# Layer 3's feed-forward: the last two tiles summed by TensorE, and the gate and up loads sent ahead of down's

## Chip, core and metric

The kernel runs on one core of a Trainium2 chip, as one launch. The metric is the device time of one execution in microseconds (us); lower is better.

## What is computed

The reference applies four layers, each with a cross-attention and a feed-forward on the normalised rows, to x of 8 x 100 tokens and 512 features. The change touches the last feed-forward alone. It sends 512 tokens to 4 of 16 experts each (expert numbers and weights are inputs), and adds the experts' weighted outputs to each token:

```python
x = hidden_states.reshape(n_tokens, h)               # 512 tokens, 512 features
flat_expert = topk_idx.reshape(-1)                   # 4 experts of each token
perm = jnp.argsort(flat_expert)
tok = jnp.repeat(jnp.arange(n_tokens), topk)[perm]
xs = x[tok]
gate = ragged_dot(xs, gate_weight^T, group_sizes)    # 16 experts, inner size 352
up = ragged_dot(xs, up_weight^T, group_sizes)
down = ragged_dot(silu(gate) * up, down_weight^T, group_sizes)
out = zeros.at[tok].add(down * w_sorted[:, None])
```

## The kernel before

The program is a chain of eight stages; each engine has one list of instructions, written out in Python, and the engines meet at semaphores. The stage here is class `ChosenFfn`, named `l3f`. Early in the program tables are made that sort the (token, expert) pairs by expert into parts of 64 rows; two parts make a tile of 128 rows, and there are 24 tiles. `rows` holds, for each lane and tile, the token of that lane (or a row beyond the tokens for an empty lane), `rows_f` the same as floats, `slot_weights` the weight.

For tile t:

- POOL gathers the 128 token rows from DRAM (`gather`) into `x_rows`, a ring of 3; TensorE turns them, ScalarE copies them to `x_turned`.
- TensorE makes gate and up for the two halves of 64 lanes, each with its own expert's weights (`pe_gate_up`, L1580), ScalarE the silu, VectorE the product `h`. TensorE turns h (L1597), VectorE copies it, and TensorE makes the down product (`pe_down`, L1607). ScalarE scales it into `y` (L1655), a ring of 2.
- POOL adds the 128 rows of `y` to two arrays in DRAM with indirect DMAs that accumulate (`add_up`, L1541), one for each half of the lanes. An add-up waits until the one before it has landed, since two tiles may add to the same token.

TensorE's list is: gate and up of t, turning of x for t + 1, down of t - 1, turning of h of t.

The weights of the second half's expert are loaded by SP into a ring of 3 (`load_ring`): 1408 KB of gate and up (L1487), 768 KB of down (L1490), from a row that SP reads from a table with `value_load` (L1485). A first half with an expert of its own gets them by POOL's indirect load into one of 2 spare places (`load_spare`, L1497); it is issued for every tile, and rows out of bounds are left out where none is needed. TensorE waits for both before a product.

SP's list in the ring: for each t, fetch the row, wait for gate and up of tile t - 2, load gate and up; wait for down of tile t - 2, load down:

```python
wait(sp, self.s("gate_up_units"), t - self.RING + 2 if t >= self.RING else 0)
sp.dma_start(self.weights[:, q, 0:self.DOWN_AT], ...)
wait(sp, self.s("d_units"), t - self.RING + 2 if t >= self.RING else 0)
sp.dma_start(self.weights[:, q, self.DOWN_AT:self.ROW], ...)
```

POOL's list in the loop: spare gate and up of t + 1, gather of t + 2, add-up of t - 1, spare down of t + 1.

At the end POOL adds up the last tile, SP loads the two arrays of sums (L1526, 1 MB each) into the place of ring 0, TensorE turns them in 32 transposes (L1637), and VectorE adds the eight results to the residual (L1687). SP sends the four pieces out (L4055).

## Time and profile before

| What | Value |
|---|---|
| median of 3 runs | 2156.8 us (2156.68 to 2157.38) |
| the profiled execution, its own time | 2163.69 us |
| its span | 2161.5 us |
| PE busy | 1973.5 us, 91% of the span |
| DVE busy | 1061.3 us, 49% |
| ACT busy | 889.4 us, 41% |
| POOL busy | 567.5 us, 26% |
| chain that ended last | PE 75%, DVE 8%, DMA 7%, ACT 4%, issue 3% |
| of it, loads of l3f gate and up | 4% |
| DMA moved | 189.22 MB, mean 88 GB/s |

The span is the time from the first to the last instruction of the profiled execution. The stage `l3f` is its last part, from some 1880 us on. Busy shares are averages over all eight stages; what limits this stage has to be read from its own windows.

### The profile page before, as it was taken

Reading aid. Unit: us, or ns where it says so; the run is one execution under the profiler, and the core shown is the slowest. Engines: PE = TensorE matmul, PEld = TensorE weight load, DVE = VectorE, ACT = ScalarE, POOL = GpSimd, SP = SyncE. Lnnn points to the kernel's source line nnn. Section 1 sums busy time; section 2 is a strip of 40 time slices with the busy share of each in tenths; the row PEclk is TensorE's granted clock in tenths of the full one; section 3 lists DMA queues with packets and bytes.
Section 4 is the critical chain, followed back from the end, with each engine's and each line's share of the span. In section 5 each row is a group of like instructions: output and inputs, shape, how many; then the busy total and the mean of one; then the engine's idle time right before and its main releaser. Section 6 shows DMA issues by size and latency. Waiting matters only on the chain.

```text
span 2161.5 us, 38438 instructions
## 1 busy us (share of the span) xinstructions
PE 1973.5 (91%) x14580; PEld 1560.8 (72%) x14580; DVE 1061.3 (49%) x2477; ACT 889.4 (41%) x1819; POOL 567.5 (26%) x416
## 2 busy tenths in 40 slices
PE   6989999996997999986899999999999999798886
PEld 6977777885446878774587777999989999633333
DVE  5546666764114366688747777333234555410111
ACT  4346666532223455566655544422253232211110
POOL 3333332322342211000031110333241110145553
PEclk9999999998998999997999999999999999899998
DMA  3200010238355221141020000222220000468895
GB/s 125 77 25 29 14 42 5 70 126 310 71 88 126 76 83 55 66 157 44 5 72 34 29 15 3 89 62 58 68 77 24 29 28 2 169 193 258 264 279 154
DMA packets 67918, 189.22 MB, mean 88 GB/s; under 512 B 15114, under 2 KB 16366, under 8 KB 62510
## 3 DMA queue, kind: packets, MB, share of 16 engines
q1 hardware_dynamic: 50606, 163.90, 22.5%
q0 software_dynamic: 17152, 23.10, 5.6%
q8 instruction: 110, 1.80, 0.3%
q14 instruction: 50, 0.41, 0.1%
HBM read 224.56 MB, written 20.91 MB: 114 GB/s over the span
## 4 chain that ended last, share of the span: by engine, by line
PE 75%; DVE 8%; DMA 7%; ACT 4%; issue 3%; SPq 1%; POOL 1%; ACTq 0%; DVEq 0%; POOLq 0%
PE psum L106 16%; PE psum L109 15%; PE psum L107 15%; DMA l3f_weights<-in_l3f_gate_up_dram 4%; PE psum L1580 4%; PE psum L900 3%; PE psum L3610 3%; PE psum L3578 2%; PE psum L2801 2%; PE psum L3596 2%; PE psum L1607 2%; PE psum L926 2%; PE psum L2447 1%; PE psum L3032 1%; PE psum L139 1%
## 5 line engine op out<-in xcount | busy, mean ns | idle before, releaser
L1580 PE MATMUL psum<-l3f_weights,l3f_x_turned 128*64 (+1 forms) x768 | 131.0, 498 | 30.6 <-issue 16.6
L1580 PEld LDWEIGHTS psum<-l3f_weights,l3f_x_turned 128*64 128x64 f32 x768 | 58.1, 148 | 94.2 <-issue 72.3
L2238 ACT ACTIVATE l2x_probs<-psum,l2x_shift 100x361 f32<-100x361 f32 x128 | 70.2, 562 | 97.3 <-DVE l2x_shift L2293 97.3
L1875 POOL TENSOR_TENSOR l2x_ctx_lo<-l2x_ctx_raw,l2x_ctx_hi 128x1448 fp32r<-128x1448 f32 x8 | 26.4, 3297 | 314.9 <-ACT l2x_ctx_hi L1883 314.9
L1676 DVE TENSOR_TENSOR l3f_h<-l3f_silu,psum 128x352 f32<-128x352 f32 x24 | 12.5, 522 | 164.4 <-ACT l3f_silu L1662 156.0
L3749 ACT ACTIVATE l0x_probs<-l0x_probs,l0x_lowest 100x361 f32<-100x361 f32 x128 | 75.2, 588 | 42.1 <-DVE l0x_lowest L3918 42.1
L106 PE MATMUL psum<-xn_hi,l2f_w_gu_hi 128*128 128x400 f32 x256 | 88.6, 346 | 1.6 <-DVE xn_lo L192 1.3
L448 POOL TENSOR_TENSOR l2f_w_gu_lo<-l2f_raw_gu,l2f_w_gu_hi 128x512 fp32r<-128x512 f32 x32 | 43.0, 1357 | 174.2 <-ACT l2f_w_gu_hi L463 174.2
L107 PE MATMUL psum<-xn_lo,l2f_w_gu_hi 128*128 128x400 f32 x256 | 87.8, 343 | 0.0
L2476 ACT ACTIVATE ln_squares<-l1x_clipped,l1x_key_shift,l1x_key_scale 128x400 f32<-128x400 f32 (+1 forms) x96 | 62.3, 712 | 51.4 <-DVE l1x_clipped L2515 51.4
L3918 DVE CUSTOM_DVE_ANT_0 l0x_probs<-psum,l0x_outside 100x361 f32<-100x361 f32 x128 | 62.9, 531 | 32.1 <-PE psum L3578 29.6
L900 PE MATMUL psum<-l0f_weights,l0f_x_turned 128*128 x160 | 74.3, 608 | 1.2 <-ACT l0f_x_turned L1042 0.8
L1662 ACT ACTIVATE l3f_silu<-psum 128x352 f32<-128x352 f32 x24 | 11.1, 464 | 154.8 <-PE psum L1580 145.3
L647 DVE TENSOR_TENSOR l2f_h<-l2f_silu,psum 128x800 f32<-128x800 f32 x16 | 15.8, 988 | 119.1 <-PE psum L109 119.1
L3610 PE MATMUL psum<-ln_squares,l0x_l_turned 128*128 128x400 f32 (+1 forms) x192 | 73.0, 516 | 0.0
L2838 ACT ACTIVATE ln_squares<-psum 64x64 f32<-64x64 f32 x128 | 28.0, 219 | 106.5 <-PE psum L2801 104.2
L109 PE MATMUL psum<-xn_hi,l2f_w_gu_lo 128*128 128x400 f32 x256 | 68.5, 344 | 0.0
L1607 PE MATMUL psum<-l3f_weights,l3f_h_turned 128*64 (+1 forms) x288 | 67.0, 600 | 0.9 <-DVE l3f_h_turned L1682 0.9
L1875 POOL TENSOR_TENSOR l1x_ctx_lo<-l1x_ctx_raw,l1x_ctx_hi 128x1448 fp32r<-128x1448 f32 x8 | 26.5, 3310 | 134.7 <-ACT l1x_ctx_hi L1883 134.7
L1875 POOL TENSOR_TENSOR l3x_ctx_lo<-l3x_ctx_raw,l3x_ctx_hi 128x1448 fp32r<-128x1448 f32 x8 | 26.4, 3295 | 126.3 <-ACT l3x_ctx_hi L1883 126.3
L2289 DVE TENSOR_REDUCE l2x_highest<-psum 100x2 f32<-100x722 f32 x64 | 57.9, 904 | 0.1
L1541 POOL DMA_INDIRECT l3f_sum_dram<-l3f_y,l3f_rows x24 | 35.0, 1460 | 86.3 <-ACT l3f_y L1655 65.7
(553 smaller groups left out, 6120.9 us busy)
## 6 DMA issues: line engine op xcount, KB each, us to landing
l3f_weights<-in_l3f_gate_up_dram SPq DMA_DIRECT2D x24, 1408.0 KB
l3f_weights<-in_l3f_down_dram SPq DMA_DIRECT2D x24, 768.0 KB
l0x_w_raw<-in_slabs_dram SPq DMA_DIRECT2D x52, 256.0 KB, 2.6
l0f_weights<-in_slabs_dram SPq DMA_DIRECT2D x8, 1536.0 KB
l1x_piece<-in_bit_w_dram SPq DMA_DIRECT2D x8, 1024.0 KB, 6.4
l1f_raw<-in_bit_w_dram SPq DMA_DIRECT2D x8, 1024.0 KB, 8.3
l2f_raw_gu<-in_slabs_dram SPq DMA_DIRECT2D x32, 256.0 KB, 2.6
l0x_ctx_raw<-in_ctx_dram SPq DMA_DIRECT2D x8, 724.0 KB, 4.2
```

The source lines that it names most:

```text
L106: pe.matmul(outs[i], weight_hi, moving[i][0], start=first, stop=False)
L107: pe.matmul(outs[i], weight_hi, moving[i][1], start=False, stop=False)
L109: mm = pe.matmul(outs[i], weight_lo, moving[i][0], start=False, stop=last)
L900: mm = pe.matmul(c.psum[:, t % 2, :], self.x_turned[:, t % 2, k, :], self.weights[:, bass.DynSlice(expert, 1), k * 512:(k + 1) * 512].rear ...
L1580: mm = pe.matmul(c.psum[lanes, bank + x, 0:self.INNER], self.x_turned[:, t % 2, k, lanes], weights, start=k == 0, stop=k == KD - 1)
L1607: mm = pe.matmul(c.psum[lanes, 6 + t % 2, :], self.h_turned[:, t % 2, k, lanes], weights, start=k == 0, stop=k == 2)
L1875: pool.tensor_tensor(self.ctx_lo[:, q, :, :], self.ctx_raw[:, :, :], self.ctx_hi[:, q, :, :], ALU.subtract).then_inc(self.s("ctx_split"), 1)
L2238: act.activation(self.probs[:, m % 2, g, :], c.psum[0:S, g, 0:C], ACT.Exp, bias=self.shift[:, g:g + 1], scale=self.SCALE, accum_out=self.t ...
L2476: act.activation(self.exps(c, m)[0:z - a, t, :], self.clipped[0:z - a, t, :], ACT.Exp, bias=shift, scale=scale).then_inc(self.s("exps"), 1)
L3610: mm = pe.matmul(c.psum[:, 6, 0:4 * S], self.l_turned[0:z - a, q, t, :], turned[0:z - a, t, :], start=t == 0, stop=t == 2)
L3749: act.activation(self.probs[:, g, :], self.probs[:, g, :], ACT.Exp, bias=self.lowest[:, g:g + 1], scale=-1.0, accum_out=self.total[:, g:g ...
L3918: dve.tensor_tensor_reduce(self.probs[:, g, :], c.psum[0:S, g, 0:C], self.outside[:, q, :], -self.SCALE, 3.0e38, ALU.add, ALU.min, self.lo ...
```

## The change

- `load_ring` is split. The gate and up load of tile t + 1 is now sent before the down load of tile t, and so is the fetch of its row number. The first three tiles, loaded ahead, keep their order.
- `ADDED` = 22: POOL adds up tiles 0 to 21 only. The last two tiles' `y` stay in SBUF. For each of them VectorE makes a table of zeros and ones (`places_of_row`): lane by token, one where the lane holds that token. TensorE multiplies `y` by it, which sums the lanes of a token and turns the result at once, into the four PSUM banks of the output.
- The arrays of sums are loaded once the add-ups of 22 tiles have landed, into a buffer of their own (`sums`), not into ring 0; the wait for the last down product is gone. VectorE joins the two arrays (4 adds of 128 x 512), TensorE multiplies the joined sums by the identity (16 matmuls) and accumulates them in the same banks. VectorE then has four adds to the residual in place of eight.

```diff
--- before.py
+++ after.py
@@ -1222,6 +1222,7 @@
     WIDE = 2 * INNER
     DOWN_AT, ROW = KD * WIDE, KD * WIDE + 3 * D
     RING, SPARE, ROWS = 3, 2, 3
+    ADDED = TILES - 2
     INNER_TILES = [(0, P), (P, 2 * P), (2 * P, INNER)]
     ROUND = 1.5 * 2.0 ** 23
 
@@ -1240,9 +1241,9 @@
         self.silu, self.h = (c.sb(own, n + x, [P, 2, self.INNER]) for x in ("_silu", "_h"))
         self.h_turned = c.sb(own, n + "_h_turned", [P, 2, 3, P])
         self.y = c.sb(own, n + "_y", [P, 2, D])
-        c.sb(own, n + "_behind_the_output_weights", [P, 5504])
+        sums = c.sb(own, n + "_sums", [P, 5504])
         self.weights = c.sb(own, n + "_weights", [P, self.RING + self.SPARE, self.ROW])
-        self.sums = self.weights[:, 0, 0:2 * self.groups * D].rearrange("p (x g d) -> p x g d", x=2, g=self.groups)
+        self.sums = sums[:, 0:2 * self.groups * D].rearrange("p (x g d) -> p x g d", x=2, g=self.groups)
 
     def early_buffers(self, c, ctx):
 
@@ -1479,13 +1480,19 @@
                            self.tile_values[:, x, :, :].rearrange("p x t -> p (x t)"), start=x == 0, stop=x == n - 1)
         mm.then_inc(c.sem("table_units"), 1)
 
-    def load_ring(self, c, sp, t):
+    def ring_row(self, sp, t):
+        return sp.value_load(self.ring_rows[0:1, t:t + 1], min_val=0, max_val=P * (self.experts - 1))
+
+    def load_gate_up(self, c, sp, t, at):
 
         q = t % self.RING
-        at = sp.value_load(self.ring_rows[0:1, t:t + 1], min_val=0, max_val=P * (self.experts - 1))
         wait(sp, self.s("gate_up_units"), t - self.RING + 2 if t >= self.RING else 0)
         sp.dma_start(self.weights[:, q, 0:self.DOWN_AT],
                      c.a["l3f_gate_up"][bass.DynSlice(at, P), :]).then_inc(self.s(f"gate_up_landed{q}"), 16)
+
+    def load_down(self, c, sp, t, at):
+
+        q = t % self.RING
         wait(sp, self.s("d_units"), t - self.RING + 2 if t >= self.RING else 0)
         sp.dma_start(self.weights[:, q, self.DOWN_AT:self.ROW],
                      c.a["l3f_down"][bass.DynSlice(at, P), :]).then_inc(self.s(f"down_landed{q}"), 16)
@@ -1508,7 +1515,9 @@
         sp.wait_ge(c.sem("tables"), 4)
         sp.dma_start(self.second_rows[:, :], self.rows[self.PART:P, :]).then_inc(self.s("second_rows"), 16)
         for t in range(self.RING):
-            self.load_ring(c, sp, t)
+            at = self.ring_row(sp, t)
+            self.load_gate_up(c, sp, t, at)
+            self.load_down(c, sp, t, at)
         for b in range(4):
             self.write_rows(c, sp, b)
 
@@ -1518,11 +1527,16 @@
             self.write_rows(c, sp, b)
         sp.dma_start(c.out[:, :, self.tokens:T], c.residual[:, :, self.tokens:T]).then_inc(c.sem("out_written"), 16)
         sp.wait_ge(self.s("x_landed0"), 16)
+        at = self.ring_row(sp, self.RING)
+        self.load_gate_up(c, sp, self.RING, at)
         for t in range(self.RING, self.TILES):
-            self.load_ring(c, sp, t)
-        sp.wait_ge(self.s("d_units"), self.TILES)
+            this, at = at, None
+            if t + 1 < self.TILES:
+                at = self.ring_row(sp, t + 1)
+                self.load_gate_up(c, sp, t + 1, at)
+            self.load_down(c, sp, t, this)
         for x in range(2):
-            sp.wait_ge(self.s(f"added_up{x}"), 16 * self.TILES)
+            sp.wait_ge(self.s(f"added_up{x}"), 16 * self.ADDED)
             sp.dma_start(self.sums[:, x, :, :], self.sum_drams[x][0:self.tokens, :].rearrange(
                 "(g p) d -> p g d", g=self.groups)).then_inc(self.s(f"sum_landed{x}"), 16)
 
@@ -1556,11 +1570,10 @@
                 self.load_spare(c, pool, t + 1, 0)
             if t + 2 < self.TILES:
                 self.gather(c, pool, t + 2)
-            if t:
+            if 0 < t <= self.ADDED:
                 self.add_up(c, pool, t - 1)
             if t + 1 < self.TILES:
                 self.load_spare(c, pool, t + 1, 1)
-        self.add_up(c, pool, self.TILES - 1)
 
     def halves(self, t, place, at, n):
 
@@ -1629,14 +1642,21 @@
             before = place
         self.pe_down(c, pe, self.TILES - 1, before)
         pe.wait_ge(self.s("h"), self.TILES)
+        pe.wait_ge(self.s("y"), self.ADDED + 1)
+        pe.wait_ge(self.s("places_of_row"), 1)
+        for m in range(KD):
+            pe.matmul(c.psum[:, m, :], self.y[:, self.ADDED % 2, m * P:(m + 1) * P], self.x_rows[:, 0, :], start=True,
+                      stop=False)
+        for g in range(self.groups):
+            pe.wait_ge(self.s("sums_joined"), g + 1)
+            for m in range(KD):
+                pe.matmul(c.psum[:, m, g * P:(g + 1) * P], self.sums[:, 0, g, m * P:(m + 1) * P], c.identity[:, :],
+                          start=False, stop=False)
         pe.wait_ge(self.s("y"), self.TILES)
-        for x in range(2):
-            pe.wait_ge(self.s(f"sum_landed{x}"), 16)
-            for m in range(KD):
-                for g in range(self.groups):
-                    mm = pe.transpose(c.psum[:, 4 * x + m, g * P:(g + 1) * P], self.sums[:, x, g, m * P:(m + 1) * P],
-                                      c.identity[:, :])
-                mm.then_inc(self.s("sum_units"), 1)
+        pe.wait_ge(self.s("places_of_row"), 2)
+        for m in range(KD):
+            pe.matmul(c.psum[:, m, :], self.y[:, (self.ADDED + 1) % 2, m * P:(m + 1) * P], self.x_rows[:, 1, :],
+                      start=False, stop=True).then_inc(self.s("sum_units"), 1)
 
     def act(self, c, act):
         act.wait_ge(c.sem("residual_ready"), self.index + 1)
@@ -1666,6 +1686,15 @@
                 out(t - 1)
         out(self.TILES - 1)
 
+    def places_of_row(self, dve, t):
+
+        into = self.x_rows[:, t - self.ADDED, :]
+        dve.wait_ge(self.s("x_units"), t)
+        for g in range(self.groups):
+            op = dve.tensor_scalar(into[:, g * P:(g + 1) * P], self.lane_ids, self.rows_f[:, t:t + 1], -float(g * P),
+                                   ALU.subtract, ALU.is_equal)
+        op.then_inc(self.s("places_of_row"), 1)
+
     def dve(self, c, dve):
         half_dve(self.norm, dve, 1)
         n = self.INNER_TILES[2][1] - self.INNER_TILES[2][0]
@@ -1680,12 +1709,17 @@
             c.apart(dve)
             dve.tensor_copy(self.h_turned[:, t % 2, 0:2, :].rearrange("p k l -> p (k l)"), c.psum[:, 5, 0:2 * P])
             dve.tensor_copy(self.h_turned[0:n, t % 2, 2, :], c.psum[0:n, 5, 2 * P:3 * P]).then_inc(self.s("h_turned"), 1)
-        for u in range(2 * KD):
-            dve.wait_ge(self.s("sum_units"), u + 1)
-            wait(dve, self.s("first_added"), u - KD + 1)
-            into = c.residual[:, u % KD, 0:self.tokens]
-            dve.tensor_tensor(into, into, c.psum[:, u, 0:self.tokens], ALU.add).then_inc(
-                self.s("first_added" if u < KD else "added"), 1)
+            if t + 1 >= self.ADDED and t + 1 < self.TILES:
+                self.places_of_row(dve, t + 1)
+        for x in range(2):
+            dve.wait_ge(self.s(f"sum_landed{x}"), 16)
+        for g in range(self.groups):
+            dve.tensor_tensor(self.sums[:, 0, g, :], self.sums[:, 0, g, :], self.sums[:, 1, g, :], ALU.add).then_inc(
+                self.s("sums_joined"), 1)
+        for m in range(KD):
+            dve.wait_ge(self.s("sum_units"), m + 1)
+            into = c.residual[:, m, 0:self.tokens]
+            dve.tensor_tensor(into, into, c.psum[:, m, 0:self.tokens], ALU.add).then_inc(self.s("added"), 1)
         dve.wait_ge(self.s("added"), KD)
         dve.nop().then_inc(c.sem("residual_ready"), 1)
```

SP, the end of the ring and the loads of the sums, before (`in_l3f_gate_up_dram` and `in_l3f_down_dram` are the weights). The `ISA` rows hold the waits; `TENSOR_LOAD` is the fetch of the row number.

```order
L1487 ISA
L1487 DMA l3f_weights<-in_l3f_gate_up_dram 128x2816
L1490 ISA
L1490 DMA l3f_weights<-in_l3f_down_dram 128x1536
L1485 TENSOR_LOAD l3f_ring_rows
L1485 ISA x2
L1487 ISA
L1487 DMA l3f_weights<-in_l3f_gate_up_dram 128x2816
L1490 ISA
L1490 DMA l3f_weights<-in_l3f_down_dram 128x1536
L1526 DMA l3f_weights<-l3f_sum_dram 128x4x512 x2
```

The same place now:

```order
L1497 ISA
L1497 DMA l3f_weights<-in_l3f_down_dram 128x1536
L1484 TENSOR_LOAD l3f_ring_rows
L1484 ISA x2
L1490 ISA
L1490 DMA l3f_weights<-in_l3f_gate_up_dram 128x2816
L1497 ISA
L1497 DMA l3f_weights<-in_l3f_down_dram 128x1536
L1497 ISA
L1497 DMA l3f_weights<-in_l3f_down_dram 128x1536
L1540 DMA l3f_sums<-l3f_sum_dram 128x4x512 x2
```

Each gate and up load, with its fetch, now stands ahead of the down load of the tile before it, and two down loads stand at the end.

TensorE, from the last down product (L1607) to the end, before:

```order
L1607 ISA
L1607 MATMUL psum<-l3f_weights,l3f_h_turned 64x512 x2
L1607 ISA
L1607 MATMUL psum<-l3f_weights,l3f_h_turned 64x512 x2
L1607 ISA
L1607 MATMUL psum<-l3f_weights,l3f_h_turned 64x512 x2
L1637 MATMUL psum<-identity,l3f_weights 128x128 x32
```

The same place now (down product L1620):

```order
L1620 ISA
L1620 MATMUL psum<-l3f_weights,l3f_h_turned 64x512 x2
L1620 ISA
L1620 MATMUL psum<-l3f_weights,l3f_h_turned 64x512 x2
L1620 ISA
L1620 MATMUL psum<-l3f_weights,l3f_h_turned 64x512 x2
L1648 MATMUL psum<-l3f_x_rows,l3f_y 128x512 x4
L1653 MATMUL psum<-identity,l3f_sums 128x128 x16
L1658 MATMUL psum<-l3f_x_rows,l3f_y 128x512 x4
```

The 32 transposes have become 4 matmuls on 512 columns, 16 on 128 and 4 on 512.

VectorE, the last two tiles and the adds, before:

```order
L1681 COPY l3f_h_turned<-psum 128x256
L1682 COPY l3f_h_turned<-psum 96x128
L1676 TENSOR_TENSOR l3f_h<-l3f_silu,psum 128x352
L1681 COPY l3f_h_turned<-psum 128x256
L1682 COPY l3f_h_turned<-psum 96x128
L1687 TENSOR_TENSOR residual<-residual,psum 128x512 x8
```

The same place now, from the table for tile 22 on:

```order
L1694 TENSOR_SCALAR l3f_x_rows<-l3f_constants,l3f_rows_f 128x128 x4
L1705 TENSOR_TENSOR l3f_h<-l3f_silu,psum 128x352
L1710 COPY l3f_h_turned<-psum 128x256
L1711 COPY l3f_h_turned<-psum 96x128
L1694 TENSOR_SCALAR l3f_x_rows<-l3f_constants,l3f_rows_f 128x128 x4
L1705 TENSOR_TENSOR l3f_h<-l3f_silu,psum 128x352
L1710 COPY l3f_h_turned<-psum 128x256
L1711 COPY l3f_h_turned<-psum 96x128
L1717 TENSOR_TENSOR l3f_sums<-l3f_sums 128x512 x4
L1722 TENSOR_TENSOR residual<-residual,psum 128x512 x4
```

The tables stand behind the copies of h of tiles 21 and 22, the joins behind the last copies, and four adds follow in place of eight.

## Rows read from the trace of the kernel before

**Rows 1.** Chain of waits, in order of time: start us, us, what.

```profile
2102.91 0.87 issue
2103.79 4.95 PE psum L1580 x32
...
2109.32 2.75 PE psum L1607 x12
...
2113.32 11.21 DMA l3f_weights<-in_l3f_gate_up_dram
2124.53 0.82 issue
2125.35 7.33 PE psum L1580 x32
```

**Rows 2.** TensorE timeline, gate and up: start us, us, operation, idle before.

```profile
1904.96 4.95 PE L1580 MATMUL psum<-l3f_weights,l3f_x_turned 128*64 x32
1913.63 4.95 PE L1580 MATMUL psum<-l3f_weights,l3f_x_turned 128*64 x32
1925.41 6.61 PE L1580 MATMUL psum<-l3f_weights,l3f_x_turned 128*64 x32 [3.04 <-issue]
...
2092.41 4.95 PE L1580 MATMUL psum<-l3f_weights,l3f_x_turned 128*64 x32
...
2112.49 4.96 PE L1580 MATMUL psum<-l3f_weights,l3f_x_turned 128*64 x32
```

**Rows 3.** Windows: us; busy PE, PEld, DVE, ACT, POOL; clock; DMA share; GB/s.

```profile
1913.80:2125.30 211.50, 182.15 (x1020) 77.28 (x1018) 23.41 (x62) 35.18 (x61) 119.38 (x101) 0.96 0.86 265
2110.50:2113.00 2.50, 2.50 (x15) 0.94 (x13) 0.29 (x1) 0.69 (x1) 0.00 (x0) 1.00 0.46 118
1914.00:1925.40 11.40, 8.38 (x51) 3.47 (x47) 1.64 (x5) 1.75 (x3) 6.59 (x6) 1.00 0.97 300
```

**Rows 4.** Waits from 1900 to 2130 us: total us, times, longest us.

```profile
PE psum L1580 <- issue: 16.3, 8, 3.0
...
PE psum L1580 <- DMA l3f_weights<-in_l3f_gate_up_dram: 13.1, 5, 4.1
```

**Rows 5.** Timeline of POOL: add-ups (L1541) and spare loads (L1497).

```profile
1905.57 1.46 POOL L1541 DMA_INDIRECT l3f_sum_dram<-l3f_y,l3f_rows  x1 [8.18 <-ACT l3f_y L1655]
...
1910.42 1.03 POOL L1497 DMA_INDIRECT l3f_weights<-in_l3f_gate_up_dram,l3f_spare_rows  x1 [0.30 <-issue]
...
2102.75 1.46 POOL L1541 DMA_INDIRECT l3f_sum_dram<-l3f_y,l3f_rows  x1 [2.57 <-DMA l3f_sum_dram<-l3f_y,l3f_rows]
...
2113.06 1.46 POOL L1541 DMA_INDIRECT l3f_sum_dram<-l3f_y,l3f_rows  x1 [3.15 <-ACT l3f_y L1655]
...
2117.91 1.03 POOL L1497 DMA_INDIRECT l3f_weights<-in_l3f_gate_up_dram,l3f_spare_rows  x1 [0.30 <-issue]
```

**Rows 6.** Chain of waits, the end of the program.

```profile
2140.52 3.67 DMA l3f_sum_dram<-l3f_y,l3f_rows
...
2144.26 7.07 DMA l3f_weights<-l3f_sum_dram
...
2158.28 0.68 DVE residual L1687
```

**Rows 7.** Timeline of the end: last down product.

```profile
2136.67 2.79 PE L1607 MATMUL psum<-l3f_weights,l3f_h_turned 128*64 x12 [0.94 <-DVE l3f_h_turned L1682]
```

**Rows 8.** Tile l3f_weights: landing of the two loads of sums.

```profile
DMA to landing us min/median/max: 7.1/7.5/7.9
```

**Rows 9.** Costliest groups of the page: xcount, busy us, mean ns, idle.

```profile
L900 PE MATMUL psum<-l0f_weights,l0f_x_turned 128*128 x160 | 74.3, 608 | 1.2 <-ACT l0f_x_turned L1042 0.8
```

**Rows 10.** Source line 1478: ns min, median, max; first and last start us.

```profile
L1478 PE MATMUL psum<-l0x_q_latent x32: 203/275/275, 63.8 to 67.2; 128*128 128x48 f32 x32
```

**Rows 11.** Groups by form on VectorE: xcount, busy us, mean ns, idle us.

```profile
L1687 DVE TENSOR_TENSOR residual<-residual,psum 128x512 f32<-128x512 f32 x8 | 5.4, 686 | 17.0 <-PE psum L1637 16.9
...
L1421 DVE TENSOR_SCALAR l0x_q_latent<-l0x_q_latent,l3f_constants 128x96 f32<-128x96 f32 x4 | 0.8, 266 | 0.0
```

## The prediction

> **What bounds the kernel now.** I read the chain of waits first. In layer 3's feed-forward the chain runs gate and up product, down product, gate and up load, next product; after the last tile it runs add-ups in DRAM, load of the sums, turning, adds [rows 1, 6]. The reader should see two separate places: a loop of tiles, and a tail.
>
> The loop. The product of tile 3 starts at 1913.63 and that of tile 23 at 2125.35 [rows 1, 2]: 211.7 us for 20 tiles, 10.59 each. A tile that waits for nothing takes 8.67 (1904.96 to 1913.63 [rows 2]). Of the 1.92 lost per tile, TensorE's idle time before the products is 16.3 + 13.1 = 29.4 us in all [rows 4]; most of the rest is products that took 6.6 to 7.3 us in place of 4.95 after an idle time [rows 1, 2]. The windows give a mean granted clock of 0.96 and a DMA share of 0.86 over these 211.5 us [rows 3]. So the DMA engines have 0.86 x 211.5 = 182 us of work, 9.1 per tile, and are idle 1.5 per tile. Neither engine nor DMA is full; the loop is made of latencies.
>
> Two chains could close it. (a) SP: the product of tile 21 ends at 2108.74 (2103.79 + 4.95), but the gate and up load of tile 23, which waits for no more than that, goes out at 2113.32, because SP first stands at the wait of down's load of tile 22 for the down product of tile 20, and then fetches an address: 4.6 us late. It lands at 2124.53 and the product starts at 2125.35 [rows 1]. Meanwhile the DMA share is 0.46 from 2110.5 to 2113 [rows 3]: 1.35 us idle. (b) POOL: tile 20's add-up goes out at 2113.06, 9.27 after the start of tile 21's product; behind it in POOL's queue is the spare gate and up load of tile 23, at 2117.91, for which TensorE waits too [rows 5]. The view names the SP load, but leaves 0.8 us of "issue" behind its landing [rows 1], so POOL's own landing may well be the last. From the add-up to the product, X, it takes 2125.35 - 2113.06 = 12.3 us. For the pair before, the add-up at 2102.75 and the product at 2112.49 [rows 2, 5], X = 9.7. With little on the DMA queues (add-up of tile 0 at 1905.57, product of tile 3 at 1913.63 without a wait [rows 2, 5]) X is at most 8.1. Over the loop two tiles take 21.2 = 9.27 + 11.9, so X is 11.9 on average, waits for earlier add-ups included.
>
> **The change, part by part.**
>
> Gate and up ahead of down, 20 tiles. No instruction is added; the load goes out up to 4.6 us earlier, the address fetch falls behind down's load, where SP has time. Down's load goes out when it did, and may land later by what is left of the gate load in front of it; it is not needed until a whole further product has run, over 8 us. (a) is gone. (b) remains, and is late next: POOL's order, its waits and its transfers are unchanged; only what they meet changes. Bounds: nothing gained if X stays 11.9 (10.59 per tile); at the other end TensorE's 8.67, or 38.3 us over 20 tiles; DMA work of 9.1 per tile stops it at 211.7 - 182 = 29.7 us. I take X = 9.7, since in that pair the gate load was already on its way when the add-up went out, as it always will be: (9.27 + 9.7) / 2 = 9.5 per tile, 190 us. **Gain 21.7 us.** The products at a low clock are in that, since the gaps before them shrink.
>
> Here a rule speaks against the change. In the trace X grows from at most 8.1 to 12.3 between few and many SP transfers. The Trainium skill, DMA: Bandwidth & Descriptors, section "Queues, rings and completion order", says that each DMA engine takes turns between rings only after a whole packet of one ring. By that rule an SP ring that is never empty makes POOL's add-ups wait for a packet at each turn; that is the second rival below.
>
> The tail. I call T the start of tile 23's product. Now the span ends 2161.5 - 2125.35 = 36.15 after T. Removed: two tiles' add-ups (four indirect DMAs), the wait for them, half of the turning (32 transposes), four of eight adds. Added: 8 table instructions on VectorE, at 266 ns for 96 columns [rows 11] some 1.1 us per tile; VectorE idles there until the next tile's silu, so they cost nothing; without that cover they would delay a tile by 1.1. On the path after it:
> - The product, down of tile 22, and down of tile 23 end at 2139.46 [rows 7] = T + 14.1, of which 2.4 is the low clock of 7.33 against 4.95 [rows 1]: T + 11.7.
> - Tile 22's rows enter by 4 matmuls of 128x128 on 512 columns. Nearest row: 160 records, 74.3 us, 20 tiles of 4 such matmuls [rows 9]: 3.7 us. T + 15.4.
> - The sums must be there. Tile 21's add-up goes out at T - 9.5 + 9.27 = T - 0.2, its second half 1.7 later, lands 3.67 after issue [rows 6] plus some 1.2 for down's load beside it: T + 6.4. The loads take 7.1 to 7.9 [rows 8]: T + 14.3. Four joins on VectorE at the adds' 0.69 [rows 11]: T + 15.0 to T + 17.1, beside TensorE's work.
> - 16 matmuls of 128 columns: 32 records in 3.6 us for 48 columns [rows 10], so 0.23 or a little more each, 3.8: T + 19.2.
> - 4 more matmuls on 512 columns for tile 23: 3.7, T + 22.9. One add behind, 0.8: T + 23.7. From the last add's end (2158.96 [rows 6]) to the end of the span 2.5: T + 26.2.
>
> **Gain 36.15 - 26.2 = 9.9 us**, 7.5 where the last product stays at the low clock. Bounds: 6, if the sums land 3 to 4 us later; 12, if the 128-column matmuls run as fast as weight loads allow.
>
> **Sum.** 21.7 + 9.9 = 31.6. The profiled execution took 2163.7 (span 2161.5); it becomes 2132.1. The median of the runs, 2156.8, is 6.9 lower: **2125 us.**
>
> **The rivals.**
> 1. Order pays in full: the DMA engines never idle, 9.1 per tile. For it: they carry 0.97 where both loads are queued, at 300 GB/s [rows 3]. Against: POOL's X would have to fall to 8.9. 29.7 + 9.9: 2117 us; with TensorE as the bound 2109.
> 2. Order pays nothing: X stays 11.9, since POOL's add-ups and the spare load behind them end the loop, not SP's load. For it: the 0.8 us behind the landing [rows 1], and POOL's own wait for an add-up of 2.57 us [rows 5]. The tail alone gives 7.5: 2149 us. This is what the rule above would make of it.
> 3. Slower: the gate load of the next tile now gets ahead of POOL's transfers once more per turn, and X grows by it. Price: 1408 KB at 300 GB/s [rows 3] is 4.8 us, for each of 10 pairs of tiles 48, less the tail's 7.5: 2197 us. It decides from 0.75 us per pair. Against: the bytes per tile are the same, and the DMA engines have 1.5 us per tile free.
>
> **How the numbers follow.** A measurement of this kernel can tell 0.2%, 4.3 us. My forecast 0.57, rival 1 0.18, rival 2 0.2, rival 3 0.05. The range reaches from between the two values of rival 1, 2111, to rival 2 with its tail, 2149. Faster by over 0.2% are all but rival 3 and its mild forms: 0.93; within 0.2% 0.03; slower 0.04.
>
> **What would show it.** SP's gate load goes out within 0.5 us after a product's end; starts of products 9.5 apart; DMA share over the loop about 0.95 and no window like 2110.5 to 2113; low-clock products rare. If the starts stay 10.4 or more apart with POOL's add-ups 12 us ahead of the product, rival 2 holds. In the tail: the loads of the sums issued before TensorE ends tile 23, the first join near T + 15, the end near T + 26. It is wrong if a down product waits for its load, or if the joins start after T + 19.

## The result, and the profile after

The changed kernel takes 2174.8 us (median of 6 runs, 2164.8 to 2178.9), the kernel before on the same chip 2156.7 (6 runs, 2155.5 to 2157.4): 1.0063 times as long, with a 95% interval of 1.0037 to 1.0088. (The ratios here and below are estimated over all runs; that of the two medians is 1.0084.) I had forecast 2125, faster. The profiled execution took 2176.7 us, its span is 2174.9, 13.4 longer than before.

The window over the loop, from the start of tile 3's product to that of tile 23, answers to [rows 3]; the second window runs from POOL's last load for tile 21 to the start of its product, the third covers that product, the fourth the 3.2 us ahead of tile 23's. Columns: us; busy PE, PEld, DVE, ACT, POOL; clock; DMA share; GB/s.

```profile
1918.85:2147.10 228.25, 190.30 (x1020) 79.93 (x1020) 23.02 (x62) 34.63 (x60) 115.49 (x98) 0.90 0.74 234
2119.70:2127.40 7.70, 3.32 (x18) 1.10 (x17) 1.14 (x3) 1.30 (x3) 5.26 (x5) 0.88 0.87 298
2127.40:2134.80 7.40, 7.40 (x33) 3.19 (x34) 0.00 (x0) 0.00 (x1) 2.66 (x3) 0.67 0.43 101
2143.90:2147.10 3.20, 3.20 (x17) 1.07 (x15) 0.52 (x1) 0.95 (x3) 1.01 (x1) 1.00 0.09 9
```

The 20 tiles take 228.3 us, 11.4 each, against 211.7 before and 190 forecast. The DMA share fell from 0.86 to 0.74, and the clock from 0.96 to 0.90. The DMA engines do not stand still while TensorE waits (0.87 in the second window); their idle time comes in the product behind the wait (0.43), since SP's next gate and up load has to wait for the end of that late product. TensorE's wait and POOL's, from 1915 to 2150 us (total us, times, longest), answer to [rows 4]:

```profile
POOL l3f_sum_dram L1555 <- ACT l3f_y L1675: 91.3, 21, 10.2
...
PE psum L1593 <- issue: 41.0, 10, 6.4
```

The waits that carried the name of SP's gate and up load are gone. What is left carries no DMA's name, and is longer than the two kinds of before together: without tile 3's own 3.0 it is 38.0 us in 9 waits, against 29.4 in 13. Of these nine the chain of waits shows two (start us, us, what):

```profile
2099.10 3.71 issue
2102.81 7.71 PE psum L1593 x32
...
2122.99 4.38 issue
2127.37 7.38 PE psum L1593 x32
```

Every second tile waits, and most products after a wait run part of the time at the lower clock, 1.2 GHz (mean granted clock 0.67 from 2127.40 to 2134.80): seven of them take 6.3 to 7.7 us in place of 4.95. These seven cost 16.3 us; the four of before cost 7.9. So the difference of the spans closes: loop 16.6 (8.6 more waiting and 8.4 more of low clock, less 0.4 that these rows leave open), tile 3 later by 5.2 (3.0 is a wait that it did not have, 2.1 came in ahead of the stage), tail shorter by 8.4. 16.6 + 5.2 - 8.4 = 13.4.

What TensorE waits for is seen by setting three engines side by side. SP, then POOL, then TensorE, timelines of the last waiting pair:

```profile
2110.71 0.33 SPq L1490 DMA_DIRECT2D l3f_weights<-in_l3f_gate_up_dram  x1
2114.02 0.33 SPq L1497 DMA_DIRECT2D l3f_weights<-in_l3f_down_dram  x1
2119.38 0.33 SPq L1490 DMA_DIRECT2D l3f_weights<-in_l3f_gate_up_dram  x1
2122.69 0.33 SPq L1497 DMA_DIRECT2D l3f_weights<-in_l3f_down_dram  x1
2134.93 0.33 SPq L1490 DMA_DIRECT2D l3f_weights<-in_l3f_gate_up_dram  x1
```

```profile
2114.85 1.47 POOL L1555 DMA_INDIRECT l3f_sum_dram<-l3f_y,l3f_rows  x1 [8.06 <-ACT l3f_y L1675]
2116.62 1.43 POOL L1555 DMA_INDIRECT l3f_sum_dram<-l3f_y,l3f_second_rows  x1 [0.31 <-issue]
2118.36 1.04 POOL L1504 DMA_INDIRECT l3f_weights<-in_l3f_down_dram,l3f_spare_rows  x1 [0.30 <-issue]
2119.71 1.01 POOL L1504 DMA_INDIRECT l3f_weights<-in_l3f_gate_up_dram,l3f_spare_rows  x1 [0.31 <-issue]
...
2128.38 1.01 POOL L1504 DMA_INDIRECT l3f_weights<-in_l3f_gate_up_dram,l3f_spare_rows  x1 [0.30 <-issue]
...
2143.93 1.01 POOL L1504 DMA_INDIRECT l3f_weights<-in_l3f_gate_up_dram,l3f_spare_rows  x1 [0.30 <-DMA l3f_sum_dram<-l3f_y,l3f_rows]
```

```profile
2114.24 4.95 PE L1593 MATMUL psum<-l3f_weights,l3f_x_turned 128*64 x32
...
2127.37 7.38 PE L1593 MATMUL psum<-l3f_weights,l3f_x_turned 128*64 x32 [4.38 <-issue]
...
2147.14 4.95 PE L1593 MATMUL psum<-l3f_weights,l3f_x_turned 128*64 x32
```

The product that waits is tile 21's (2127.37; tiles 22 and 23 start at 2138.47 and 2147.14). Its gate and up load by SP went out at 2110.71, 16.7 us earlier. What is young is POOL's spare gate and up load for tile 21, at 2119.71, 7.7 us ahead. And 0.33 us ahead of it stands SP's load of 1408 KB for tile 22, whose product starts only at 2138.47. This 0.33 is no accident: SP's load waits for the end of tile 20's product (2114.24 + 4.95), POOL's comes 4.86 after an add-up, and that add-up follows the down product just ahead of tile 20's product. So the two meet in the same way ahead of eight of the nine waits, 0.31 to 0.33 us apart (2048.91 and 2049.24, 2069.45 and 2069.78). Ahead of the ninth, tile 11's and the longest (6.4 us), SP's load goes out at 2003.76, within the 1.01 us of POOL's instruction from 2003.73. Before, SP's last gate load stood 4.6 us ahead of POOL's spare load (2113.32 and 2117.91 [rows 1, 5]).

The same rows say why only every second tile waits. POOL's spare load for tile 22 needs nothing of the late product and goes out at 2128.38; SP's load for tile 23 has to wait for the end of the late product and follows 6.6 us later, at 2134.93. In the ten tiles between the waits it follows 2.6 to 8.4 us later, and no product waits. Tile 23 is the test of this: there is no tile 24, so no gate and up load meets its spare load at 2143.93, the DMA share is 0.09, and the product starts on time at 2147.14. The spare load had landed after 3.2 us at most; in the nine waits it was 6.2 to 9.7 us old when the product began.

The tail, timeline of TensorE and of the joins (T is 2147.14):

```profile
2157.20 2.80 PE L1620 MATMUL psum<-l3f_weights,l3f_h_turned 128*64 x12 [2.05 <-DMA l3f_weights<-in_l3f_down_dram,l3f_spare_rows]
2159.93 3.70 PE L1648 MATMUL psum<-l3f_x_rows,l3f_y 128*128 128x512 f32 x8
2163.47 3.73 PE L1653 MATMUL psum<-identity,l3f_sums 128*128 128x128 f32 x32
2167.04 3.60 PE L1658 MATMUL psum<-l3f_x_rows,l3f_y 128*128 128x512 f32 x8
```

```profile
2160.82 2.50 DVE L1717 TENSOR_TENSOR l3f_sums<-l3f_sums 128x512 f32<-128x512 f32 x4 [4.88 <-DMA l3f_sums<-l3f_sum_dram]
...
2170.67 0.69 DVE L1722 TENSOR_TENSOR residual<-residual,psum 128x512 f32<-128x512 f32 x1 [0.17 <-PE psum L1658]
```

The span ends at T + 27.8 (36.15 before, 26.2 forecast). The tables of ones took 0.93 and 1.04 us for four and lay beside other work.

### The profile page after: what moved, and what is told of

It is laid out like the page before. It is cut to its first block, busy times and chain, and to the rows that moved or that the text cites. A ratio compares the mean times of both kernels' runs of the same rounds, so it can differ in the third digit from the quotient of the medians.

```text
span 2174.9 us, 38469 instructions
## 1 busy us (share of the span) xinstructions
PE 1984.8 (91%) x14596; PEld 1562.7 (72%) x14596; DVE 1063.5 (49%) x2485; ACT 889.3 (41%) x1819; POOL 562.5 (26%) x412
## 4 chain that ended last, share of the span: by engine, by line
PE 79%; DVE 8%; ACT 4%; issue 4%; DMA 3%; SPq 1%; POOL 1%; POOLq 0%; ACTq 0%; DVEq 0%
PE psum L106 16%; PE psum L109 14%; PE psum L107 14%; PE psum L1593 6%; PE psum L900 3%; PE psum L3644 3%; PE psum L1620 3%; PE psum L3612 2%; PE psum L2835 2%; PE psum L3630 2%; PE psum L926 2%; PE psum L3066 1%; PE psum L2481 1%; DMA l0f_weights<-in_slabs_dram 1%; PE psum L139 1%
## 5 line engine op out<-in xcount | busy, mean ns | idle before, releaser
L1593 PE MATMUL psum<-l3f_weights,l3f_x_turned 128*64 (+1 forms) x768 | 137.0, 516 | 42.2 <-issue 41.3
L1705 DVE TENSOR_TENSOR l3f_h<-l3f_silu,psum 128x352 f32<-128x352 f32 x24 | 12.5, 521 | 180.1 <-ACT l3f_silu L1682 180.1
L1620 PE MATMUL psum<-l3f_weights,l3f_h_turned 128*64 (+1 forms) x288 | 67.0, 600 | 2.0 <-DMA l3f_weights<-in_l3f_down_dram,l3f_spare_rows 2.0
## 6 DMA issues: line engine op xcount, KB each, us to landing
l0f_weights<-in_slabs_dram SPq DMA_DIRECT2D x8, 1536.0 KB, 17.5
```

The lines of the kernel that those rows point to most:

```text
L1593: mm = pe.matmul(c.psum[lanes, bank + x, 0:self.INNER], self.x_turned[:, t % 2, k, lanes], weights, start=k == 0, stop=k == KD - 1)
L1620: mm = pe.matmul(c.psum[lanes, 6 + t % 2, :], self.h_turned[:, t % 2, k, lanes], weights, start=k == 0, stop=k == 2)
```

## The experiments

Two theories stood after the result. **A**: POOL's spare gate and up load, behind the add-ups in POOL's list, is what TensorE waits for; the new SP order puts another tile's load in front of it. **The rival**: the loop is slower for another reason that came with the change (the tail's part of it, SP's own transfers, or TensorE's clock). Other letters in the expectations stand for forms of this rival. All runs are compared with the kernel before on their own chip, whose medians were 2157.7, 2158.3 and 2160.5 us. Brackets behind a ratio hold its 95% interval.

### The two halves of the change apart

SP's new order alone, on the kernel before with its old tail (the loop; `load_ring` is split as in the change):

```diff
-        for t in range(self.RING, self.TILES):
-            self.load_ring(c, sp, t)
+        at = self.ring_row(sp, self.RING)
+        self.load_gate_up(c, sp, self.RING, at)
+        for t in range(self.RING, self.TILES):
+            this, at = at, None
+            if t + 1 < self.TILES:
+                at = self.ring_row(sp, t + 1)
+                self.load_gate_up(c, sp, t + 1, at)
+            self.load_down(c, sp, t, this)
```

> The changed order of SP's loads alone, with the old tail. Theory A (the gate load of tile t + 1 goes out just ahead of POOL's spare gate load for tile t, which carries no weights in nearly every tile but whose landing TensorE waits for, and which now lands only with that gate load): the loop is as slow as in the changed kernel, product of tile 23 some 228 us after that of tile 3 (211.7 before), low-clock products 7 or so; total 2174.8 + 8.4 = about 2183 us. Theory B (the loss comes from the new buffer, tables or tail, not the order): about 2157 us. Theory C (rival 2 of the prediction, the order neither helps nor hurts): 2157 us as well.

Measured: 2185.4 us (4 runs, 2182.1 to 2193.0), ratio 1.0129 [1.0099, 1.0159]. The loop, 1918.00 to 2147.66, takes 229.7 us:

```profile
1918.00:2147.60 229.60, 188.67 (x1020) 79.49 (x1020) 22.17 (x58) 34.57 (x60) 115.63 (x98) 0.90 0.74 233
```

```profile
PE psum L1594 <- issue: 43.9, 10, 6.4
```

Clock, DMA share and waits are those of the changed kernel (43.9 us with tile 3's own 3.0 us, as 41.0 there). The whole loss is the order's: 27.8 us of the medians on one chip.

The new tail alone, with SP's old order:

```diff
-        at = self.ring_row(sp, self.RING)
-        self.load_gate_up(c, sp, self.RING, at)
         for t in range(self.RING, self.TILES):
-            this, at = at, None
-            if t + 1 < self.TILES:
-                at = self.ring_row(sp, t + 1)
-                self.load_gate_up(c, sp, t + 1, at)
-            self.load_down(c, sp, t, this)
+            at = self.ring_row(sp, t)
+            self.load_gate_up(c, sp, t, at)
+            self.load_down(c, sp, t, at)
```

> The changed tail alone: the last two tiles summed by TensorE, loads of gate and up and down in the old order. Theory A: loop as before (211 to 213 us from the product of tile 3 to that of tile 23), the tail 7.5 to 9.9 us shorter, total 2147 to 2149 us. Theory B: the loop is slow here too, product of tile 23 over 220 us after that of tile 3, total about 2175 us.

Measured: 2154.7 us (10 runs, 2146.3 to 2161.9), ratio 0.9992 [0.9977, 1.0008]: less than expected. The profiled execution was the shortest one, 2146.3, with a loop of 204.4 us (1913.00 to 2117.35, before 211.7) and a tail of T + 27.15. So the tail is as short as in the changed kernel in this trace, but the ten times lie up to 15.6 us apart, which buries a gain of 8 us. That it is the loop which differs from run to run is not shown: one execution has a trace. The tail's worth can't be read from this pair.

### POOL's spare load moved, under both SP orders

The spare gate and up load and the gather go out one tile earlier, ahead of the add-up. The spare load for tile t + 2 takes the place of tile t's, so it waits there for tile t's product:

```diff
+        self.load_spare(c, pool, 1, 0)
+        self.gather(c, pool, 2)
         for t in range(self.TILES):
-            if t + 1 < self.TILES:
-                self.load_spare(c, pool, t + 1, 0)
             if t + 2 < self.TILES:
-                self.gather(c, pool, t + 2)
+                self.load_spare(c, pool, t + 2, 0)
+            if t + 3 < self.TILES:
+                self.gather(c, pool, t + 3)
             if 0 < t <= self.ADDED:
                 self.add_up(c, pool, t - 1)
```

> The changed kernel, with POOL's spare gate load and gather one step earlier in its list: the spare gate load of tile t + 2 and the gather of tile t + 3 stand ahead of the add-up of tile t - 1 (each still waits for the product or turning that frees its place). Theory A: the spare gate load no longer stands behind the add-ups and behind the gate load of the next tile; it lands beside its own tile's gate load, 5 us or more before it is needed. The loop falls to 8.9 to 9.5 us per tile, product of tile 23 178 to 190 us after tile 3; total 2125 to 2137 us. If instead the DMA engines' work or the add-ups' chain bounds the loop (rival D), it stays above 10 us per tile and the total above 2147 us.

Measured: 2119.3 us (4 runs, 2117.5 to 2122.0), ratio 0.9819 [0.9799, 0.9839]. Better than expected: the products of tiles 3 to 23 start 8.67 us apart without a wait.

```profile
1913.60:2087.20 173.60, 173.58 (x1023) 73.92 (x1022) 23.65 (x64) 35.02 (x61) 116.03 (x97) 1.00 0.99 313
```

```profile
2079.11 1.47 POOL L1555 DMA_INDIRECT l3f_sum_dram<-l3f_y,l3f_rows  x1 [2.12 <-ACT l3f_y L1677]
...
2088.40 1.45 POOL L1555 DMA_INDIRECT l3f_sum_dram<-l3f_y,l3f_rows  x1 [4.74 <-ACT l3f_y L1677]
2090.15 1.42 POOL L1555 DMA_INDIRECT l3f_sum_dram<-l3f_y,l3f_second_rows  x1 [0.30 <-issue]
2091.88 1.05 POOL L1504 DMA_INDIRECT l3f_weights<-in_l3f_down_dram,l3f_spare_rows  x1 [0.30 <-issue]
```

The first fence is the window over the loop: TensorE is busy throughout at a clock of 1.00. The second is the end of POOL's timeline; the down product of tile 23 waits 2.9 us for the last spare load in it, 2091.88, behind an add-up again.

The two loads still meet. In this trace SP's gate and up load goes out 0.3 to 1.0 us ahead of POOL's spare load in each tile from tile 5 on (2066.30 and 2066.97, for one), as in the changed kernel. But that spare load belongs to the tile after next: its product starts 11.5 us later, where TensorE came to the nine waits of the changed kernel 3.3 us after the spare load went out. What pays is the lead, not that the meeting is avoided.

The same POOL list with SP's old order:

> The changed tail, SP's loads in the old order, and POOL's spare gate load and gather one step earlier. Theory A: what is left is SP's own late gate load (4.6 us behind the product), which lands 9 to 11 us after its issue; the loop gains little over the old one, 9.9 to 10.4 us per tile, total 2133 to 2146 us, slower than the same list of POOL with the new order of SP. Rival D (DMA work or the add-ups bound the loop): the same time as the changed tail alone, 2148 us.

Measured: 2137.1 us (4 runs, 2134.5 to 2140.2), ratio 0.9902 [0.9879, 0.9925], 9.48 us per tile (189.6 from 1914.01 to 2103.58), less than the 9.9 expected at least.

```profile
1914.00:2103.60 189.60, 174.72 (x1023) 75.16 (x1022) 25.02 (x70) 35.29 (x61) 115.88 (x97) 1.00 0.95 291
```

```profile
PE psum L1591 <- issue: 14.6, 14, 1.8
```

Here the waits that I had called chain (a), SP's late gate load, are what is left: 14 of at most 1.8 us. The view gives them no name; ahead of the last, at 2103.58, SP's load went out 9.7 us before and POOL's spare load 13.5. With the new tail throughout, the four kernels are:

| | SP old order | SP new order |
|---|---|---|
| POOL's spare load behind the add-up | 2154.7 | 2174.8 |
| POOL's spare load ahead of it | 2137.1 | 2119.3 |

The same edit of SP's list costs 20 us in one row and gains 18 in the other (three of the four were measured on one chip, 2174.8 on that of the result; with the old tail the loss is 27.8 us on one chip). The spare load's place decides its sign.

### Nothing moved, but SP's load held back

If it is the meeting of two loads 0.33 us apart that costs, holding SP's back a little must help. In the changed kernel the gate and up load of tile t got one wait more, on the copy of the turned x:

```diff
+        wait(sp, self.s("x_turned"), t if t > self.RING else 0)
```

> The changed kernel, but SP's gate load of tile t also waits for ScalarE's copy of the turned x of tile t - 1, which ends some 1.3 us after the product it waited for. Everything else, the place ahead of down's load too, is as in the changed kernel. Theory A (what costs is that the gate load is issued 0.3 us ahead of POOL's empty spare load and is served first, 2119.38 against 2119.71 us in the changed kernel's trace): now the spare load is issued about 1 us ahead of it; part or all of the delay goes, the loop falls from 11.4 to between 9 and 10.6 us per tile, total 2120 to 2158 us. Rival E (an earlier gate load slows POOL's transfers by sharing the DMA engines with them, whichever comes first): 1 us later changes little, 11.0 us per tile or more, total 2166 us or more.

Measured: 2143.6 us (10 runs, 2132.0 to 2158.3), ratio 0.9925 [0.9894, 0.9957]. In the trace, of the slowest of these runs, POOL's load now goes out first, at 2100.93, and SP's 1.3 us behind it. The third row is the product for which that spare load is:

```profile
2100.93 1.01 POOL L1505 DMA_INDIRECT l3f_weights<-in_l3f_gate_up_dram,l3f_spare_rows  x1 [0.30 <-issue]
```

```profile
2102.20 0.01 SPq L1491 DMA_DIRECT2D l3f_weights<-in_l3f_gate_up_dram  x1
```

```profile
2108.43 7.17 PE L1594 MATMUL psum<-l3f_weights,l3f_x_turned 128*64 x32 [4.22 <-issue]
```

So going out first by 1.3 us is not enough by itself: the product still waits 4.2 us, and its spare load is 7.5 us old. In this trace ten spare loads have SP's load 0.9 to 1.3 us behind them. Four had landed after 4.0 us or less; six were 5.3 to 8.8 us old when their product ended its wait. That chance may be why the ten times lie 26 us apart, which one trace cannot show.

And held back until the down product, which is 3.5 us after the product's end in the trace (4.6 in the kernel before, 0.2 in the changed one):

```diff
+        wait(sp, self.s("d_units"), t - self.RING + 1 if t > self.RING else 0)
```

> The changed kernel, but SP's gate load of tile t also waits for the down product of tile t - 3, the wait that down's load of tile t - 1 has; gate load first, down's load right behind. The gate load goes out 3.3 us after the product, against 4.6 before the change and 0.2 in the changed kernel. Theory A: the spare load is ahead of the gate load in most pairs of tiles; loop 9.3 to 10.4 us per tile, total 2126 to 2153 us. Rival E: between before and the changed kernel, about 11 us per tile, total near 2165 us.

Measured: 2146.7 us (10 runs, 2144.1 to 2153.7), ratio 0.9946 [0.9929, 0.9963]. SP's load goes out 3.0 us or more behind POOL's, and the 14 waits, of at most 2.6 us, end on spare loads 4.4 to 6.3 us old. Issuing a load later made the kernel 31 and 28 us faster by the medians (on two chips whose kernels before differ by 1.6 us), which no theory gives in which SP's own loads were what TensorE waited for.

### The spare loads left out

For tiles 1 to 23 the spare loads and TensorE's waits for them are gone, and with them the weights of a first half that has an expert of its own:

> The changed kernel without POOL's spare loads (gate and up, and down) for tiles 1 to 23 and TensorE's waits for them; those of tile 0 stay. It leaves out the weights of a first half with an expert of its own, where a tile has one. Theory A: the loop is free of the only late landing, 8.7 to 9.2 us per tile; total 2112 to 2128 us. Rival E or the add-ups' chain as the bound: the add-ups, the gather and both loads of SP are unchanged, so the loop stays above 10 us per tile, total above 2145 us.

Measured: 2118.5 us (4 runs, 2116.0 to 2120.7), ratio 0.9814 [0.9774, 0.9854]. SP's order, the add-ups and the gathers are those of the changed kernel, though on POOL the gathers no longer have spare loads ahead of them:

```profile
1913.90:2087.30 173.40, 173.40 (x1021) 73.83 (x1020) 23.61 (x64) 34.87 (x61) 76.06 (x59) 1.00 0.97 314
```

How much those loads carry is in the page's part on DMA queues (packets, MB, share), first of the kernel with POOL's list moved, which still has them all, then of this one:

```profile
q0 software_dynamic: 16832, 22.58, 5.5%
```

```profile
q0 software_dynamic: 10208, 22.55, 5.5%
```

46 loads less take away 6624 packets, 144 each, and 0.03 MB. With these inputs the spare loads carry next to nothing. What was expensive was waiting for their completion, not sending them: the version with POOL's list moved sends all of them and is as fast.

### What the tail is worth on a loop without waits

The kernel with SP's new order and POOL's list moved, but with the old tail (24 add-ups, 32 transposes, eight adds):

> The old tail with the new order of SP and POOL's spare gate load one step earlier: against the run with the same loop and the changed tail (2119.3 us) it prices the tail on a loop that always waits for nothing. The prediction's working gave 7.5 us for the tail at the full clock (9.9 with 2.4 of a last product at the low clock): 2127 us. In the traces the changed tail took 27.8 and 28.5 us against 36.15 - 2.4 = 33.8 before: 5.3 to 6 us, 2125 us. If the tail is worth nothing, 2119 us.

Measured: 2125.7 us (4 runs, 2121.7 to 2126.4), ratio 0.9839 [0.9798, 0.988]. The new tail gains 6.4 us of the medians, but they are from two chips, and the two ratios, 0.9839 and 0.9819, have intervals that overlap: the gain is not clear of noise. By the two traces the spans differ by 7.1 us. 4.1 of it is in the tail (2122.8 - 2090.18 = T + 32.6 against 2115.7 - 2087.18 = T + 28.5), and 2.5 is in this kernel's loop, nearly all of it one wait for a spare down load; the rest lies ahead of the loop.

The new tail has the 2.9 us wait for a spare down load. With that load sent ahead of the last add-up:

```diff
+            if t == self.TILES - 2:
+                self.load_spare(c, pool, t + 1, 1)
             if 0 < t <= self.ADDED:
                 self.add_up(c, pool, t - 1)
-            if t + 1 < self.TILES:
+            if t + 1 < self.TILES - 1:
                 self.load_spare(c, pool, t + 1, 1)
```

> The version with POOL's spare gate load ahead of the add-up, and now the spare down load of tile 23 ahead of the add-up of tile 21 too. Theory (the down product of tile 23 is late by POOL's order again, 2.9 us in that version's trace): the wait is gone and the down product ends near T+11.7 instead of T+13.6; tile 22's rows, the 16 small matmuls and the last four follow some 1.9 us earlier if the joins keep up. The add-up goes out about 1 us later, so the joins start near T+14.5 to T+15. Total 1 to 2 us less than that version's 2119.3: 2117.5 to 2118.5. Rival (the sums end the tail): the first small matmul waits for the join, T+15 or later, and the time stays at 2119 to 2120. Loop: 8.67 per tile in both.

Measured: 2118.3 us (5 runs, 2116.6 to 2125.0), ratio 0.9803 [0.9781, 0.9825], not to be told from 0.9819. The time lies in the theory's range, but it can't decide. The trace (T is 2094.70) is of the slowest of the five, 2125.0 us, and its loop is not the one expected: 181.4 us, 9.07 per tile, with waits before down products (5.1 us for spare down loads) that the version before it did not have. For the tail it says more; the rows are TensorE's and VectorE's timeline:

```profile
2103.65 2.80 PE L1624 MATMUL psum<-l3f_weights,l3f_h_turned 128*64 x12 [0.94 <-DVE l3f_h_turned L1715]
2106.38 3.70 PE L1652 MATMUL psum<-l3f_x_rows,l3f_y 128*128 128x512 f32 x8
2111.71 3.84 PE L1657 MATMUL psum<-identity,l3f_sums 128*128 128x128 f32 x32 [1.64 <-DVE l3f_sums L1721]
```

```profile
2110.96 2.50 DVE L1721 TENSOR_TENSOR l3f_sums<-l3f_sums 128x512 f32<-128x512 f32 x4 [7.46 <-DMA l3f_sums<-l3f_sum_dram]
```

The down product is on time, at T + 8.95, but the joins start at T + 16.3 and not at T + 14.1, and the small matmuls wait 1.64 us for them. The rival of that run is what this trace shows: two things end within 2 us of each other there, and taking one away shows the other.

### The gather's share

In the version with POOL's list moved the gather had moved too. With the spare load alone moved:

```diff
+        self.load_spare(c, pool, 1, 0)
         for t in range(self.TILES):
-            if t + 1 < self.TILES:
-                self.load_spare(c, pool, t + 1, 0)
             if t + 2 < self.TILES:
                 self.gather(c, pool, t + 2)
+                self.load_spare(c, pool, t + 2, 0)
```

> The changed kernel with POOL's spare gate and up load alone one step earlier: it is issued ahead of the add-up, but behind the gather, which keeps its tile and its place. Theory A (only the place of the spare load behind the add-up costs): as with both moved, 8.7 per tile without waits, 2118 to 2122 us. Rival (the gather of the token rows, issued two tiles ahead, had been late as well and its move gave part of the gain): waits of TensorE for the gathered rows or the turned x, 9.0 or more per tile, 2126 us or more.

Measured: 2128.0 us (5 runs, 2125.4 to 2130.9), ratio 0.9851 [0.9828, 0.9874], 9.15 us per tile (183.0 from 1915.44 to 2098.47). I had put my theory on 2118 to 2122; the rival was right.

```profile
PE psum L1602 <- DMA l3f_x_rows<-l3f_x_dram,l3f_rows: 6.2, 7, 1.2
PE psum L1602 <- issue: 2.3, 4, 0.8
```

The gathered rows are late next. From the loop of the changed kernel (228.3) down to 173.6 the two steps are 45 us for the spare load and 9 for the gather.

## Why the prediction was wrong

**Step that failed: X.** I had seen POOL's chain (b), and that it is late next once (a) is gone. Then I wrote "I take X = 9.7, since in that pair the gate load was already on its way when the add-up went out, as it always will be". The load that is on its way in the new order is not the one of the product that waits but the next tile's, and it is sent anew just ahead of POOL's spare load. X in the pairs that wait is 11.0 to 14.6, 12.4 on average over nine (2114.85 to 2127.37 is 12.5); before, 10.2 to 12.3, 11.0 over twelve. The term beside X failed too: from a product that waits to the next add-up I took 9.27 us, which holds at the full clock; behind a product at the low clock it is 12.04 (2102.81 to 2114.85). One pair, 2102.75 to 2112.49, was a thin base: its product did not wait at all, so its 9.7 was what TensorE's own list took, and no more than a bound for a landing that nobody waited for.

**Rival 3 was the right mechanism, at a smaller price.** It said that the gate load of the next tile gets ahead of POOL's transfers once more per turn. I priced it at a whole load, 4.8 us a pair, and gave it 0.05. Measured, X grew by 1.4 us, and the pair became 1.7 us longer (16.6 us over 10 pairs, half of it low clock), above the point of 0.75 us that I had worked out. "Against: the bytes per tile are the same" was no argument: the spare load carries nearly no bytes, and is late all the same.

**DMA work.** "The DMA engines have 0.86 x 211.5 = 182 us of work" took the busy share for an amount of work. The window of before held 265 x 211.5 = 56.0 MB, and that of the version with POOL's list moved 313 x 173.6 = 54.3 MB in 0.99 x 173.6 = 172 us; the changed kernel's 53.4 MB came with 0.74 x 228.3 = 169 us. So the bound was 6% too high, in equal parts since that window held more bytes and since a MB took 3.25 us of share there and 3.16 here: 8.6 us per tile in place of 9.1, and the loop ran at 8.67, with TensorE and the DMA engines both full. So once POOL is out of the way the loop runs at the TensorE bound that stands behind rival 1's 2109. The time, 2119.3, is still nearer its 2117: I had taken 6.9 us off the profiled execution to reach the median, and of that kernel the profiled execution, 2117.5, lies below the median.

**The gain of the order.** 21.7 us was forecast. With POOL's list moved the order gains 17.9 (2137.1 to 2119.3). Chain (a) was there as read, and hidden under (b). That 17.9 is near 21.7 is luck: the forecast let (b) shrink by itself, and (b) had to be moved by another edit.

**Low clock.** "The products at a low clock are in that, since the gaps before them shrink" went the other way, seven in place of four, 8.4 us. They followed the waits, which had become fewer and longer: thirteen waits of up to 4.1 us before had four such products in the loop, nine of 2.9 to 6.4 us after had seven.

**The tail.** 9.9 us forecast, with 7.5 for a full clock in the last product. By the traces T + 36.15 became T + 27.8, a gain of 8.4, which holds the 2.4 of a low-clock product that the last tile did not have this time; on a loop without waits it is 4.1. Of the 1.6 us missed, the late end of the down product of tile 23 is 1.1: it waited 2.05 us for its spare load, which went out behind the add-up of tile 21 (I had named such a wait among what would show the forecast wrong, and had not costed it). The end behind the last add is 1.0, 3.5 in place of 2.5 us. The matmuls (3.5, 3.6, 3.6 against 3.7, 3.8, 3.7) took 0.5 back. The joins started at T + 13.7 and took 0.63 each, not 0.69.

**The rule.** Rival 2 went with the Trainium skill, DMA: Bandwidth & Descriptors, section "Queues, rings and completion order": a DMA engine takes turns between rings, and only after a whole packet of one. A nearly empty load of 144 packets that is 6.2 to 9.7 us old when TensorE goes on agrees with such turns behind a load of 1408 KB, and so does the one of at most 3.2 us where the DMA share was 0.09. That it is the turns, and not another way in which the two loads hold each other up, no run here separates.

**What the method missed.** The order of instructions on SP was read well, but against the wrong neighbour. POOL's list laid beside SP's, with what releases each entry, would have shown it from the trace of before. The spare load goes out 4.85 us behind an add-up that follows the down product (2113.06 to 2117.91 [rows 5]). SP's new gate load goes out 0.2 us behind the end of the product in between, and there that end is 2112.49 + 4.96 = 2117.45 [rows 2]: 2117.6, 0.3 us ahead of the spare load. Two tiles earlier it is the same, 2092.41 + 4.95 + 0.2 = 2097.6 against a spare load at 2097.87.

## What to carry to other kernels

When a load is sent earlier, ask what else goes out within a microsecond of its new moment, on every queue, and who waits for that: here a small transfer that was waited for lost more beside a large one than the large one gained. A transfer that carries nothing still has to complete, so give it a lead: put it in its queue ahead of whatever waits, and a tile early. Holding the large one back by 1 to 3 us helped too, but with waits left and times that spread. And where two late things sit behind one another, price the edit with the second one in place: the same line was worth -20 and +18 us.

## What was not expected of the hardware

- 46 indirect loads that carry 0.03 MB together have 144 packets each, and TensorE waited for them until 6.2 to 9.7 us after their issue while SP's loads ran (nine waits; 5.3 to 7.4 in the kernel before, twelve). With the DMA share at 0.09 one had landed after 3.2 us at most.
- The busy share of the DMA engines per MB hardly depends on how full they are: 3.16 us at a share of 0.74 and at 0.99, 3.25 at 0.86, 3.26 at 0.95 (SP's old order with POOL's list moved), 3.09 at 0.97 (no spare loads). As a bound it is good to a few per cent: by 3.25 us a MB the 54.3 MB of the fast loop make 8.8 us per tile, and it ran at 8.67; taken per tile, without the MB, it was 9.1.
- A loop that waits spreads: ten runs of one kernel lay between 2146.3 and 2161.9, ten of another between 2132.0 and 2158.3. The kernel before lay within 1.9 us in the six runs of the result, and within 17.5 us in 19 on another chip. The versions with POOL's list moved, or without spare loads, lay within 4.4 to 8.4 us in four or five runs each.

What stays open: why the waits have lengths from 2.9 to 6.4 us, though eight of the nine meetings are 0.31 to 0.33 us apart; why a spare load that goes out 1.3 us ahead of SP's is sometimes in time and sometimes not; and what part of its time is spent before its packets run.
